# Second attention layer: softmax sums at 128x64, inverted there and spread by TensorE

## The reference

```python
Q = Q * cos + _rotate_half(Q) * sin
K = K * cos + _rotate_half(K) * sin
scores = jnp.einsum('bhtd,bhsd->bhts', Q, K) / jnp.sqrt(jnp.asarray(hd, Q.dtype))
attn = jax.nn.softmax(scores, axis=-1)
context = jnp.einsum('bhts,bhsd->bhtd', attn, V)
context = context.transpose(0, 2, 1, 3).reshape(B, T, D)
return context @ Wo + bo
```

## Time and profile before

| what | value |
|---|---|
| time, median of 3 runs | 1751.86 us (1750.91 to 1755.05) |
| the profiled execution's own time | 1748.74 us |
| its span, first to last instruction | 1746.9 us |
| mean granted TensorE clock | 0.92 |
| PE, DVE, ACT, POOL busy | 79%, 67%, 55%, 62% of the span |
| second attention, scores of iterations 1 to 31 | 893.38 to 1273.31 us |

### The profile page before, as it was taken

How to read it: one execution, slowest core, us unless ns; L and a number is a source line. 1 busy time by engine, 2 the same in 40 slices (tenths; PEclk the granted TensorE clock), 3 DMA queues, 4 the chain that set the end, 5 groups by cost and what they waited for, 6 DMA issues and landing times. The chain is left out here.

```text
span 1746.9 us, 56992 instructions
## 1 busy us (share of the span) xinstructions
PE 1372.5 (79%) x20302; PEld 1064.4 (61%) x20303; DVE 1176.1 (67%) x3431; ACT 957.2 (55%) x2418; POOL 1091.4 (62%) x1338
## 2 busy tenths in 40 slices
PE   5999999739677777777268888888854799999784
PEld 3677777514377767767156666666632578777663
DVE  5788888689577777777268888888869222322165
ACT  2677777617454545545067676777735344444332
POOL 3777777500377777776577777777210777777773
PEclk9999999959899999999688999999975899999987
DMA  4211111000144444443242222222100111111174
GB/s 161 89 45 36 45 36 46 21 7 1 26 109 105 108 103 109 106 106 104 64 158 66 63 63 62 61 63 59 33 14 1 51 54 55 54 54 54 55 231 136
DMA packets 136994, 122.85 MB, mean 70 GB/s; under 512 B 27675, under 2 KB 121915, under 8 KB 136123
## 3 DMA queue, kind: packets, MB, share of 16 engines
q0 software_dynamic: 26624, 56.35, 12.7%
q1 hardware_dynamic: 110078, 64.47, 12.1%
q10 hardware_dynamic: 192, 0.67, 0.1%
HBM read 80.24 MB, written 41.18 MB: 70 GB/s over the span
## 5 line engine op out<-in xcount | busy, mean ns | idle before, releaser
L1539 POOL DMA_INDIRECT arena<-expert_rows,token_of_slot x432 | 416.0, 963 | 283.8 <-issue 221.9
L419 POOL DMA_INDIRECT arena<-slot_results,slot x256 | 250.3, 978 | 95.7 <-issue 73.6
L1930 DVE TENSOR_TENSOR arena<-bank,arena 128x352 f32<-128x352 f32 x144 | 75.5, 524 | 222.6 <-ACT arena L1909 222.6
L1863 PE MATMUL bank<-W,arena 128*128 x576 | 198.7, 469 | 0.9 <-ACT arena L1921 0.9
L593 DVE TENSOR_REDUCE mx<-bank 128x8 f32<-128x512 f32 x256 | 158.4, 681 | 33.1 <-PE bank L907 31.9
L1774 POOL DMA_INDIRECT token_results<-arena,slot x144 | 141.2, 980 | 53.3 <-issue 43.7
L445 POOL TENSOR_TENSOR arena<-arena,fixed 128x1024 f32<-128x1024 f32 x64 | 121.3, 1916 | 44.6 <-ACT arena L733 44.6
L725 ACT ACTIVATE arena<-bank 128x512 f32<-128x512 f32 x256 | 131.3, 598 | 25.0 <-PE bank L944 25.0
L1637 PE MATMUL bank<-arena 128*128 128x128 f32 x1152 | 144.0, 279 | 0.0
L1877 PEld LDWEIGHTS bank<-W,arena 128*128 128x128 f32 (+1 forms) x864 | 115.5, 192 | 38.2 <-issue 30.8
L1637 PEld LDWEIGHTS bank<-arena 128*128 128x128 f32 x1152 | 136.9, 195 | 0.2
(11 more groups left out here) (220 smaller groups left out, 3379.0 us busy)
## 6 DMA issues: line engine op xcount, KB each, us to landing
slot_results<-arena SPq DMA_DIRECT2D x72, 256.0 KB, 2.4
arena<-in_ctx SPq DMA_DIRECT2D x64, 128.0 KB
expert_rows<-arena SPq DMA_DIRECT2D x64, 128.0 KB
arena<-token_results SPq DMA_DIRECT2D x32, 256.0 KB, 3.8
arena<-expert_rows,token_of_slot POOLq DMA_INDIRECT x432, 2.6
W<-in_w SPq DMA_DIRECT2D x4, 1032.0 KB, 5.1
X<-in_x SPq DMA_DIRECT2D x32, 128.0 KB, 2.2
arena<-slot_results,slot POOLq DMA_INDIRECT x256
```

Source lines behind the costliest of these rows:

```text
L419: nc.gpsimd.indirect_dma_start(out=gb[i.par][:, to:to + D], out_offset=None, in_=ys, in_offset=bass.IndirectOffsetOnAxis(ap=slot[:, at, k: ...
L1539: nc.gpsimd.indirect_dma_start(out=XE[n % R][:, c * ROW:(c + 1) * ROW], out_offset=None, in_=ts, in_offset=bass.IndirectOffsetOnAxis(ap=to ...
L1863: last = nc.tensor.matmul(H_[2 * r + u][:, 0:F1], XT[i.par][:, c * P:(c + 1) * P], W1a[:, bass.ds(x_e, 1), u * F1:(u + 1) * F1], start=Tru ...
```

## The change

In layer 1 alone, the sums are collected once for each head and not once for each column. 32 matmuls of 64 columns (L993 in the changed kernel) with a new constant `den_at` take the place of 8 of 256 columns, and leave the sums of four sequences as 128x64 in the columns from 256 of `O_`. DVE inverts 128x64 into `rec` (`invert_sums`). ACT copies the values 128x256 from `O_` to a new SBUF tile `sums` (`values_copied`), after DVE has inverted. PE then spreads `rec` to 128x256 by four matmuls with the new constant `den_to` (`scales_spread`, L1012), over the columns that held the sums, after ACT has copied. DVE multiplies `sums` by these 256 columns (`scale_values`), now after the rotary work. The tile `fixed` grows by 768 columns. Layer 0 is as before. Cut: the unpacking of the names of the constants.

```diff
@@ -40,7 +40,7 @@
 E1, K1, F1 = 8, 2, 352
 F1_BLOCKS = [128, 128, 96]
 GROUP = 4
-FIXED = {"ident": P, "cos": S, "sin": S, "gate_w": E0 + E1, "max_to": 4 * S, "den_of": 64, "bias_t": 9, "head_of": 4,
+FIXED = {"ident": P, "cos": S, "sin": S, "gate_w": E0 + E1, "max_to": 4 * S, "den_of": 64, "den_at": 256, "den_to": 512, "bias_t": 9, "head_of": 4,
          "gate_b": E0, "bias_r": 2 * D}
 FLAG = 65536
 W1_0 = 2 * F0 + 2
@@ -304,7 +304,7 @@
         weights_out = sem("weights_out")
         names = ("stats_a", "moments_a", "eps_a", "rstd_a", "normed", "cx_psum", "cx", "v_psum", "vbd", "qk_psum",
                  "qk", "rot_psum", "rot", "keys", "queries", "rope", "kbd", "qbd", "score_psum", "score_max", "mx_psum",
-                 "mx_here", "t_psum", "probs", "o_psum", "o_recip", "o_normed", "wo_psum",
+                 "mx_here", "t_psum", "probs", "o_psum", "o_recip", "o_copied", "o_scales", "o_normed", "wo_psum",
                  "added", "stats_r", "moments_r", "pool_r", "rstd_r", "mean_r", "moments_both", "offsets", "rstd_both", "scaled_both", "rows_added", "t_ready", "tt_psum", "tt",
          s = {n: sem(n) for n in names}
@@ -322,7 +322,8 @@
             Mk = None if layer else carve2(2 * S, BF16)
             mxT = carve(2 * P)
             Pt = [carve(512) for _ in range(UNITS)]
-            rec = carve(2 * D)
+            rec = carve(S if layer else 2 * D)
+            sums = carve(2 * D) if layer else None
             aoT = carve2(2 * D)
             t = carve2(2 * D)
             tT = carve2(2 * D)
@@ -634,6 +635,17 @@
                         dve.wait_ge(s["o_recip"], i.g + 1)
                         nc.vector.tensor_tensor(aoT[q], O_[:, 0:2 * D], rec, ALU.mult).then_inc(s["o_normed"], 1)
 
+                    def invert_sums(i):
+
+                        dve.wait_ge(s["o_psum"], i.g + 1)
+                        nc.vector.reciprocal(rec, O_[:, 2 * D:2 * D + S]).then_inc(s["o_recip"], 1)
+
+                    def scale_values(i):
+
+                        dve.wait_ge(s["o_scales"], i.n + 1)
+                        nc.vector.tensor_tensor(aoT[i.par], sums, O_[:, 2 * D:4 * D], ALU.mult
+                                                ).then_inc(s["o_normed"], 1)
+
                     def weigh(i, buf, src, b0, b1, tab, done):
 
                         for h, b in ((0, b0), (1, b1)):
@@ -689,7 +701,7 @@
                             for r in range(UNITS):
                                 score_unit(i, r)
                         if on(-1):
-                            divide(pv)
+                            invert_sums(pv)
                         if on(1):
                             dve.wait_ge(s["qk_psum"], nx.g + 1)
                             if not (isinstance(nx.n, int) and nx.n < 1):
@@ -697,6 +709,8 @@
                                 dve.wait_ge(s["rope"], nx.n)
                             weigh(nx, QKe, P_, bq, bk, cos, "qk")
                             rotate(nx)
+                        if on(-1):
+                            scale_values(pv)
                         if on(3):
                             combine(i.at(3))
                         if on(-3):
@@ -816,6 +830,11 @@
                                 X[:, bass.ds(i.n * 2 + j, 1), :].rearrange("p i d -> p (i d)"), ACT.Identity,
                                 bias=mm[:, j:j + 1], scale=rs[:, j:j + 1])
                         last.then_inc(s["normed"], 1)
+
+                    def values_copied(i):
+
+                        act.wait_ge(s["o_recip"], i.g + 1)
+                        nc.scalar.activation(sums, O_[:, 0:2 * D], ACT.Copy).then_inc(s["o_copied"], 1)
 
                     def maxima_copied(i):
 
@@ -858,6 +877,8 @@
                             normalise(ex)
                         if on(-4):
                             keep_top(i.at(-4))
+                        if on(-1):
+                            values_copied(i.at(-1))
                         if on(0):
                             maxima_copied(i)
                         if on(-3):
@@ -964,6 +985,17 @@
                                         O_[32 * r:32 * r + 32, 64 * sq:64 * sq + 64], Vp[i.par][:, at:at + 32],
                                         Pt[r][:, 128 * sq + 64 * j:128 * sq + 64 * j + 64],
                                         start=(j == 0), stop=(j == 1), skip_group_check=True)
+                        if layer:
+                            for sq in range(4):
+                                for j in range(2):
+                                    at = (2 * sq + j) * 32
+                                    for r in range(UNITS):
+                                        last = nc.tensor.matmul(
+                                            O_[32 * r:32 * r + 32, 256:256 + S], den_at[:, at:at + 32],
+                                            Pt[r][:, 128 * sq + 64 * j:128 * sq + 64 * j + 64],
+                                            start=at == 0, stop=at == 224, skip_group_check=True)
+                            last.then_inc(s["o_psum"], 1)
+                            return
                         for j in range(2):
                             for r in range(UNITS):
                                 last = nc.tensor.matmul(
@@ -972,6 +1004,14 @@
                                     Pt[r].rearrange("p (t j q) -> p t j q", t=4, j=2)[:, :, j, :],
                                     start=(j == 0), stop=(j == 1), skip_group_check=True)
                         last.then_inc(s["o_psum"], 1)
+
+                    def scales_spread(i):
+
+                        pe.wait_ge(s["o_copied"], i.n + 1)
+                        for sq in range(4):
+                            last = nc.tensor.matmul(O_[:, 256 + S * sq:256 + S * sq + S], den_to[:, P * sq:P * sq + P],
+                                                    rec, start=True, stop=True, skip_group_check=True)
+                        last.then_inc(s["o_scales"], 1)
 
                     def inputs(i):
 
@@ -1085,6 +1125,9 @@
                             pe.wait_ge(s["added"], pv.g)
                         if on(0):
                             maxima(i)
+                        if on(-1):
+                            scales_spread(pv)
+                        if on(0):
                             turned(i)
                         if on(-3):
                             if on(1):
@@ -1994,6 +2037,10 @@
              "max_to": -(np.arange(P)[:, None] % 32 == np.arange(4 * S)[None, :] // S).astype(np.float32),
              "den_of": (np.arange(64)[None, :] // 32 * 2 + np.arange(P)[:, None] // S
                         == np.arange(64)[None, :] % 32 // HD),
+             "den_at": np.arange(256)[None, :] % 16 == (np.arange(256)[None, :] // 64 * 4
+                                                        + np.arange(256)[None, :] // 32 % 2 * 2 + np.arange(P)[:, None] // S),
+             "den_to": np.arange(P)[:, None] == (np.arange(512)[None, :] % P // 32 * 32 + np.arange(512)[None, :] // P * 4
+                                                 + np.arange(512)[None, :] % 32 // HD),
              "bias_t": np.stack([i["L0_xattn_bq"], i["L0_xattn_bk"], i["L1_xattn_bq"], i["L1_xattn_bk"],
                                  i["L1_xattn_bq"][half], i["L1_xattn_bk"][half], i["L0_xattn_bv"], i["L1_xattn_bv"],
                                  i["L0_ffn_norm_scale"]], axis=1),
```

More of the change, by code:

```diff
@@ L132, in part_of @@
             return fixed[:, at:at + FIXED[name]]
-        ident, cos, sin, gate_w, max_to, den_of, bias_t, head_of, gate_b = (
-            part_of(n) for n in ("ident", "cos", "sin", "gate_w", "max_to", "den_of", "bias_t", "head_of", "gate_b"))
+        ident, cos, sin, gate_w, max_to, den_of, den_at, den_to, bias_t, head_of, gate_b = (
+            part_of(n) for n in ("ident", "cos", "sin", "gate_w", "max_to", "den_of", "den_at", "den_to", "bias_t", "head_of", "gate_b"))
         bias_r = part_of("bias_r").rearrange("p (l d) -> p l d", l=2)
```

## The result

| what | before | after |
|---|---|---|
| time, median (5 runs each, side by side) | 1755.05 us (1750.91 to 1756.25) | 1787.73 us (1781.97 to 1790.23) |
| ratio, with its 95% interval | | 1.0187 [1.0171, 1.0204] |
| the profiled execution's own time, its span | 1748.74, 1746.9 us | 1785.12, 1783.3 us |
| mean granted clock | 0.920 | 0.918 |
| second attention, 30 periods | 379.93 us | 412.30 us |

What follows compares the result with a forecast made beforehand. A loop of waits through ACT and PE sets the second attention's period; 25.7 us over 30 periods plus 1.0 at the start, drain 0, add 26.7 to 1751.86: 1778 us, own range 1767 to 1790, stated range 1757 to 1795 (0.8).

Steps and rivals of the forecast that it cites:

- The loop through ACT and TensorE: Second attention: waits between ACT and PE, from scores to next scores, set the period, 11.93 us at full clock.
- without a gain beyond 0.30: At expert rows L1019: DVE's path shortens by 1.57 us, but its gain is capped at 0.30 us by PE's path.
- The sums at no cost: PE's 64 loads take 0.87 us like L963's, ending about 998.2, covered by the wait for ACT until 998.37: nothing.
- TensorE's wait of 0.30 us for ACT's copy: Before the spread: PE's maxima have their loads in at 1000.34, ACT's copy lets the spread begin at 1000.64.
- The spread: PE, ahead of the transposed scores: eight loads take 1.00 us, bounds 0.11 to 1.2, plus issue gap 0.17.
- The periods: Second attention: 12.93 us at full clock, 14.15 at 0.87, 13.54 for the kind between.
- The kinds 11, 10 and 9: The 30 periods stay 11 at full clock, 10 at 0.87 to 0.89, 9 at 0.93 to 0.95: +25.7 us.
- The start: Kernel start: `fixed` grows by 384 KB, 1.0 us, between 0 (hidden) and 1.1.
- The drain: Behind the last iteration: 1.2 us of inversion is traded for the copy and spread, 0.
- DVE is the bound: Rival at L1019: DVE's path alone decides, the spread falls into PE's spare time, period 11.63 at most: 1722 us, chance 0.05.
- the hidden spread: Rival: spread costs 0.11 us, periods 12.04 at full clock, 13.34 and 12.69 in the others: 1753 us, chance 0.06.
- both cases of the clock: Rivals for the 30 periods: clock never slow, 1761 us, chance 0.14; slow in every period, 1797 us, chance 0.13.

Runs made afterwards that it cites:

- the run with the late spread: Changed kernel with the spread on PE behind the next values and the multiplication on DVE behind the added expert results: 1743.38 us, 0.9952.
- the filler: Inputs' transposition issued twice in the second attention: on the late spread 1732.24 us, 0.9883; with the weights' loads behind the loop as well 1735.29 us, 0.9891.

## Why the prediction was right, point by point

**The loop through ACT and TensorE** is shown: taking the spread off it gave 1.1 to 1.2 us a period back at full clock (0.2 of it by the sums), doubling the spread added 0.81 to 0.85, and a quarter of it gave 0.65 to 0.67 back. What the prediction did not see is the second loop through DVE, at about 12.0 us. So "without a gain beyond 0.30" was right for the place where the change put things, but with the spread off the loop DVE's 1.2 us do count: in the run with the late spread the loop's periods at full clock are all but one between 11.8 and 12.0, where the earlier trace rows has 11.93 and 12.59. That the shorter inversion makes this difference is argued from DVE's timeline, not tried by itself.

**DVE's inversion** took 0.55, as said, and DVE waited for the projections in place of being waited for.

**The sums at no cost** was mis-sized by 0.2 to 0.3 us: their 64 loads took 1239.98 - 1238.65 = 1.33 us, not the 0.87 of L963. They outlast their cover and move the projections to 3.27 us after the scores, from 2.98 in the second half and from 3.06 in the first (where the run with the old sums has them). It is not the loads alone that are slow: with the spread late the same 64 take 0.97 to 1.03 us. Why they are slower in the changed kernel's order stays open.

**TensorE's wait of 0.30 us for ACT's copy** did not show, since the maxima came later by as much. With the old sums it did, as 0.24. Two errors of opposite sign, so the spread began at 5.30 us, at 5.22 in the half that the working was made on, and not at 5.25. That they cancel is luck.

**The spread** is 1.03 us from its first load to the transposed scores, where the working has 1.00 and an issue gap of 0.17 that did not come. From the transposed scores to L1059 it was 1245.20 - 1243.04 = 2.16 us and not 2.01. These two cancel as well. The eight loads by themselves take 0.97.

**The periods:** L1059 at 8.49 us (8.43 forecast), 13.1 us at full clock (12.93) and 14.2 in the slow ones (14.15). In the half that the working followed, at full clock, it is 978.70 - 970.27 = 8.43 and 12.94 us, in the run with the weights moved. The mechanism was right; that it fits to 0.01 us rests on the errors that cancel.

**The kinds 11, 10 and 9** were wrong, as the working warned that they might be: in the loop 13 periods are at 0.98 or 0.99 and 13 at 0.87 to 0.90, and nothing is between. In sum it is nearly the same, +23.8 us for 26 periods against 25.7 x 26 / 30 = 22.3, which is partly luck: two other runs with a spread on this loop were nearly all fast or nearly all slow.

**The start:** the load of `fixed` took 0.6 us longer (6.9 against 6.3), and the first layer's first scores came at 21.15 us against 20.14, the 1.0 forecast. By the second attention 0.3 of it was left.

**What was left out** are the edges. The drain behind the last scores, put at 0, cost 3.2 us (29.02 against 25.81): the inversion's gain is there, but TensorE has little else to do and waits for ACT's copy, 0.97 us before 1312.26 and 1.18 before 1321.43, and the spread follows each time. The last of the 30 periods cost 3.5 us; it ran at 0.80, where it had been at 1.00. The first three cost 5.05 with the two stops, which went when the weights' loads were moved, but for one of 1.01 us. For these four periods the forecast holds 25.7 x 4 / 30 = 3.4 us, so the edges are 3.2 + 8.55 - 3.4 = 8.4 of the 9.7 us by which the sum is off in the profiled execution (36.4 against 26.7). They are most of why the median rose by 32.7 us and not by 26.7.

**The rivals.** "DVE is the bound" (1722 us) fell as stated; so did the hidden spread and, in this kernel, both cases of the clock. The experiments show that the clock cases were real dangers: nearly all fast with the spread twice, nearly all slow with a quarter of it. That the share of slow periods follows TensorE's idle time was an assumption of mine, in the forecast as in the rivals: in the loop a stand of 1.7 to 1.8 us came ahead of every period, and 13 of the 26 still ran at 0.98 or 0.99.

## What to carry to other kernels

Ask of every added operation which loop it stands on, and of every removed one whether that loop contains it: the same spread made the kernel 1.9% slower at one place of TensorE's order, and a few instructions later the same work ran 0.5% faster than before. Where periods differ in granted clock, compare only periods at one clock to judge an edit, and expect the clock to change the sum: here less work on TensorE gained nothing in the total (1.0177 against 1.0187) and useless work ran faster (1732.24 against 1743.38 us). Look also at the second-longest loop, since it is what an edit meets as soon as it shortens the first.

## What the runs showed of the hardware

The granted clock moved with small edits in either direction. A quarter of the spread, with less work, had nearly all periods at 0.87 or 0.88; the spread twice had nearly all at 1.00; the transposition of the inputs a second time took the late spread from 1743.38 to 1732.24 us. A slow period of the changed kernel costs 1.26 us against the same half of the loop at full clock (14.20 against 12.94; with the spread twice 15.21 against 13.95), and it is paid behind a stand of TensorE, in the scores, values and sums. The fall does not follow from that stand alone: it is 1.73 us ahead of a period at 0.90 and 1.72 ahead of the next one at 0.98. What decides between the two was not settled.

TensorE stopped for 0.9 to 5.1 us at a time (the longest with a quarter of the spread, before 913.63) in the middle of a group, waiting for nothing that the program names. In the twelve traces there are 29 such stops in the second attention, all in the iterations ahead of the loop, in its first pass or behind it. The transfer of weights has a part in it: with it moved, the two stops of 2.4 us went and two shorter ones, of 1.01 and 1.35, were there; with the filler and the late spread, one of 3.90 came at its new place. It is neither needed, as the stop at 947.58 shows, nor enough, as the second period of the run with the old sums shows.

The traces hold more about it. They list DMA packets of a kind called instruction; in the changed kernel, from 900 to 930 us:

```profile
q8 instruction: 4, 0.07, 0.9%
```

Each of them is of 16 KB, and each of the 29 stops ends 1.25 to 1.60 us after one of them has ended: the stop before 911.32 after the packet from 908.84 to 909.72, the one before 925.40 after 922.92 to 923.90, the one before 913.63 after 911.21 to 912.16, the one before 947.58 after 945.21 to 946.18. From 964 to 1266 us, where the loop's instructions come again, the changed kernel has no packet of this queue and no such stop. That TensorE waited there for its next instructions is my reading of these times and of the queue's name: no run tried it, and the traces do not name the engine that a packet was for. Most packets go without a stop: in the changed kernel, of the 12 of this queue from 895 to 960 us, two go with one.
